# Rotation, first part, rest, second part and last part of queries and keys get a step each in an attention and expert-routing kernel

## What is computed

```python
q, k, v = (heads(wq, bq), heads(wk, bk), heads(wv, bv))
q = _apply_rope(q, cos, sin)
k = _apply_rope(k, cos, sin)
att = jnp.einsum('bhtd,bhsd->bhts', q, k) * scale
att = jnp.where(causal, att, jnp.float32(-jnp.inf))
att = jax.nn.softmax(att, axis=-1)
y = jnp.einsum('bhts,bhsd->bhtd', att, v)
...
x = _layernorm(x + attention)
probs = softmax(x @ gate_w.T); top 8 of 32 experts, weights normalised
x = _layernorm(x + sum over the 8 of  w_e * (u * silu(g)) @ down_w[e].T)
```

## Time and profile before

| | |
|---|---|
| median of three runs | 2444.79 us |
| lowest, highest | 2440.87, 2453.05 us |
| the profiled execution's own time | 2436.65 us |
| its span in the trace | 2434.7 us |
| mean granted TensorE clock | 0.941 of full speed |
| busy over the span | PE 83%, DVE 67%, ACT 64%, POOL 46% |

### The profile page before, as it was taken

The page is one execution under the profiler, slowest core; times in us unless marked ns, Lnnn a source line. Parts: engine busy times, 40 slices in busy tenths (PEclk is TensorE's granted clock), DMA queues, the critical chain, the costliest instruction groups (busy, mean ns, idle before and its releaser), DMA issues.

```text
span 2434.7 us, 57839 instructions
## 1 busy us (share of the span) xinstructions
PE 2024.7 (83%) x18031; PEld 1451.6 (60%) x18031; DVE 1641.3 (67%) x3492; ACT 1561.8 (64%) x3171; POOL 1125.8 (46%) x1110
## 2 busy tenths in 40 slices
PE   4888888888888888888779999998898997989780
PEld 3454544444544444445448788887787886778660
DVE  4677777777777677777635655655677775776673
ACT  2566665656645555555547677777787886878670
POOL 1005345543455345554353013002777757775775
PEclk7899999999989999989989999999899999999995
DMA  5456566656667666657847679888999998999893
GB/s 174 131 163 218 177 216 226 228 184 193 207 218 259 223 205 226 219 183 239 279 169 266 195 247 330 265 271 283 324 355 314 321 307 283 323 315 293 281 298 113
DMA packets 330817, 591.90 MB, mean 243 GB/s; under 512 B 47168, under 2 KB 168416, under 8 KB 328416
## 3 DMA queue, kind: packets, MB, share of 16 engines
q1 hardware_dynamic: 251232, 400.17, 50.6%
q0 software_dynamic: 53760, 159.45, 19.3%
q10 hardware_dynamic: 25536, 28.58, 3.6%
HBM read 326.68 MB, written 299.50 MB: 257 GB/s over the span
## 4 chain that ended last, share of the span: by engine, by line
PE 32%; POOL 18%; DVE 14%; issue 13%; DMA 11%; ACT 6%; SPq 4%; ACTq 1%; DVEq 1%; POOLq 0%
POOL stacks L759 16%; DMA qk_parts<-pbuf 4%; DVE mn L1484 3%; PE ps L876 3%; PE ps L935 3%; PE ps L1008 3%; PE ps L923 3%; PE ps L901 3%; PE ps L989 2%; PE ps L991 2%; PE ps L990 2%; DMA stacks<-qk_parts 2%; SPq L591 2%; PE ps L825 2%; ACT work L1143 2%
## 5 line engine op out<-in xcount | busy, mean ns | idle before, releaser
L1143 ACT ACTIVATE pT<-ps 128x1024 f16<-128x1024 f16 (+4 forms) x1408 | 825.5, 599 | 419.7 <-PE ps L925 287.4
L743 POOL DMA_INDIRECT x_sorted<-xhl,idx x512 | 532.4, 1040 | 415.2 <-DVE xhl L1555 263.7
L759 POOL DMA_INDIRECT stacks<-y_sorted,idx x512 | 522.7, 1021 | 396.7 <-DMA y_sorted<-work 196.3
L1484 DVE TENSOR_REDUCE mn<-ps 128x1 f32<-128x512 f32 (+3 forms) x704 | 416.0, 633 | 93.4 <-PE ps L903 89.0
L989 PE MATMUL ps<-pT,gu_hi 128*128 128x256 f16 x1536 | 425.4, 277 | 14.3 <-issue 7.9
L990 PE MATMUL ps<-pT,gu_hi 128*128 128x256 f16 x1536 | 424.8, 277 | 0.0
L991 PE MATMUL ps<-pT,gu_lo 128*128 128x256 f16 x1536 | 424.3, 276 | 0.0
L923 PE MATMUL ps<-stacks 99*128 99x512 bf16 (+3 forms) x1024 | 310.2, 317 | 67.1 <-ACT pT L1143 44.7
L901 PE MATMUL ps<-stacks 96*128 96x512 bf16 (+3 forms) x1024 | 290.8, 317 | 62.6 <-DMA stacks<-qk_parts 35.8
L1051 PE MATMUL ps<-dn,vx 128*128 x768 | 212.1, 276 | 80.6 <-DVE vx L1647 54.3
L925 PE MATMUL ps<-maskk,identb 128*128 128x128 bf16 x1024 | 232.9, 228 | 0.0
(11 more groups left out here) (229 smaller groups left out, 3634.0 us busy)
## 6 DMA issues: line engine op xcount, KB each, us to landing
y_sorted<-work SPq DMA_DIRECT2D x288, 256.0 KB
stacks<-qk_parts SPq DMA_DIRECT2D x128, 384.0 KB
x_sorted<-zeros_h SPq DMA_DIRECT2D x132, 288.0 KB
stacks<-x_sorted SPq DMA_DIRECT2D x88, 288.0 KB, 4.0
y_sorted<-yev SPq DMA_DIRECT2D x96, 256.0 KB
qk_parts<-pbuf SPq DMA_DIRECT2D x62, 384.0 KB
pT<-x_sorted SPq DMA_DIRECT2D x70, 288.0 KB
pbuf<-x_sorted SPq DMA_DIRECT2D x70, 288.0 KB, 5.3
```

The costliest lines, as they stand in the source:

```text
L743: pool.indirect_dma_start(xsort[g][:, :], bass.IndirectOffsetOnAxis(ap=at, axis=0), xhl_rows[:, t, :], None).then_inc(s_scat, 16)
L759: pool.indirect_dma_start(yg[:, r, k, :].bitcast(I32), None, ysort[g][:, :], bass.IndirectOffsetOnAxis(ap=at, axis=0)).then_inc(s_yg[r], 16)
L1143: return nc.scalar.activation(o, i, f, **k)
L1484: V.tensor_reduce(mn[:, tt, h0:h0 + nh], ps[:, odd_bank("max", at, m), 0:nh * n].rearrange("p (a n) -> p a n", a=nh), axis=AX.X, op=ALU.ma ...
```

## The change

The five operations get a step each. For queries: rotation in 3, first copy in 4, rest in 5, second copy in 6, last part in 7, write in 8 (before: 3, 4, 4, 5, 5, 6). For keys: 9, 10, 11, 12, 13, 14 (before: 8, 9, 9, 10, 10, 12). The keys' projection and `rope` go from steps 7 and 8 to 8 and 9, the load of the reciprocals from 10 to 11 and that of the numerators from 11 to 12. No instruction is added, removed or resized.

```diff
-SLOT_K = (7, 8)
-SLOT_PARTS = ((3, 4, 5, 6), (8, 9, 10, 12))
+SLOT_K = (8, 9)
+
+SLOT_PARTS = ((3, 4, 5, 6, 7, 8), (9, 10, 11, 12, 13, 14))
...
-SLOT_REC_IN = 10
-SLOT_NUM = 11
+SLOT_REC_IN = 11
+SLOT_NUM = 12
...
-                        if e == SLOT_PARTS[n][3] and nxt:
+                        if e == SLOT_PARTS[n][5] and nxt:
                             write_parts(i + 1, n)
...
-                        if e in SLOT_PARTS[n][1:3] and nxt:
-                            part_copy(i + 1, n, SLOT_PARTS[n][1:3].index(e))
+                        if e in SLOT_PARTS[n][1:4:2] and nxt:
+                            part_copy(i + 1, n, SLOT_PARTS[n][1:4:2].index(e))
...
-                            if e == SLOT_PARTS[n][1]:
+                            if e == SLOT_PARTS[n][2]:
                                 rest(i + 1, n)
-                            if e == SLOT_PARTS[n][2]:
+                            if e == SLOT_PARTS[n][4]:
                                 last_part(i + 1, n)
```

## The result

With the change the kernel takes 2487.07 us (median of 4 runs, 2469.44 to 2495.57), the kernel before beside it 2445.86 (4 runs): 1.016 times as long, 95% interval 1.009 to 1.022. Run again later beside 11 runs of the kernel before, it took 2481.26 against 2444.99, 1.0145 (1.0127 to 1.0164). So the change costs 36 to 41 us. The forecast was +10, and both times lie near or beyond the upper end of its range, 2482. The profiled execution took 2479.76 us with a span of 2477.8, 43 us over that of before.

The account below looks back on a forecast made before the run. It took the loop through the keys' write, the stack's load and step 20 to bound ten batches. 16 - 5 + 1 - 2 = +10 us on 2444.8 gave 2454.8 us, range 2422 to 2482.

Parts of the forecast that it names:

- What bounds the kernel: In ten batches, the loop of step 20, keys' parts, their write and the stack's load; PE waits 18.4 us for such loads.
- What the change removes: The ping-pong: PE's 4.44 us wait in step 10 and DVE's 2.19 before `last_part`; 2 to 2.5 us a batch if engine-bound.
- Queries' write: In batch 6 it starts 3.2 us later than at 534.97, at 538.1, behind two more steps' reductions.
- Its landing: The queries' write takes 9.9 us, landing at 548.0 in batch 6, so ACT's first keys copy waits 1.6 us.
- Rival B: Slower: step 8's 768 KB stack load ahead of the queries' write delays its landing 2 to 3 us; +30, 2475; 22%.
- Keys' write: In batch 6 it starts 3.1 us later, saves 1.4 beside fewer scatters, and lands 1.7 us later.
- the sum: Ten batches x 1.6 us = 16, less 5, plus 1, less 2: +10 us.
- credit of -5 for step 24: In five batches (3, 7, 10, 11, 14) a later stack only eats into step 24's wait of 1.0 us: -5.
- Numerators: Their load, now behind the row maxima, holds the division up 1 to 2 us; costed at nothing, step 20 not being due.
- The keys' projection takes as long a step later: Moved one step on, it costs nothing, PE being busy there in both.
- Rival C: Faster: the keys' write escapes the scatters and lands 2.1 us earlier; ten times, -21, 2424; 18%.
- Rival D: Nothing: bytes moved between steps 8 and 20, not the moment of issue, set the stack's arrival; 2445; 15%.

Follow-up runs that it names:

- g1: Kernel before with the keys' steps as changed (9 to 14), queries at their old steps, numerators' load at step 11: 2451.43 us against 2443.73, 1.0027.
- g2: Kernel before with only the keys' projection and everything behind it one step on, old ping-pong kept, write at 13: 2456.26 us against 2443.73, 1.0045.
- f3: Changed kernel with the queries' parts and write back at their old steps (3, 4, 4, 5, 5, 6): 2464.53 us against 2444.99 for the kernel before, 1.0077.
- g4: Kernel before with the keys' ping-pong undone (rotation 8, copies and parts 9 to 11), write kept at step 12: 2438.74 us against 2443.73, 0.9975.
- f1: Changed kernel with the queries' write issued ahead of step 8's stack load, same kernel as e1: 2479.30 us against 2444.99 for the kernel before, 1.0139.
- e1: Changed kernel with the queries' write issued ahead of step 8's stack load: 3323.27 us against 3342.85 for the kernel before, 0.994.
- e4: Changed kernel with the numerators' load back at step 11: 3328.61 us against 3342.85 for the kernel before, 0.995.
- f2: Changed kernel with the keys' first two parts in a buffer of their own in 12 of 14 batches: 2463.62 us against 2444.99, 1.0068.
- g3: Kernel before with only the keys' six pieces spread over steps 8 to 13 from the old start, write at 13: 2442.75 us against 2443.73, 0.9992.
- h1: Changed kernel with the numerators' load at step 11, e4 again: 3291.91 us against 3301.31 for the kernel before, 0.9965.
- h2: Changed kernel with the queries at their old steps, f3 again: 3291.94 us against 3301.31 for the kernel before, 0.9972.
- e3: Changed kernel with the queries at their old steps (3, 4, 4, 5, 5, 6): 3333.60 us against 3342.85 for the kernel before, 0.996.

## Why the prediction was wrong

**What bounds the kernel** was read rightly, as far as it went: the loop over the keys' write and step 20. PE's waits for stacks went from 18.4 to 41.7 us, where "towards 45" was forecast. What was overlooked is a second deadline on the same queue, step 12, for which the step-8 load comes just in time before the change (0.9 us of waits in all) and no longer does when the steps in front of it get shorter (g1, g2, f3: 39 to 45 us).

**What the change removes** held. PE's wait in step 10 of batch 6 is 1.15 us instead of 4.44 ("2 or less"), and DVE's wait before `last_part` is gone (28.5 us over all batches before); it now waits for ACT's first copy before `rest` instead, 39.7 us in 7 places. And the first of these comes of the later projection and copy (g2), not of the end of the ping-pong (g4).

**Queries' write** held: it starts 8.0 us before the end of the keys' rotation in batch 6 (546.41 to 554.38) where I had 538.1 to 546.4, 8.3.

**Its landing** is the step that failed. I took batch 8's 9.9 us as the price of the write, unchanged. It took 14.7 in batch 6 and 12.8 on average (9.2 before). Instead of 1.6 us, the copy stood 561.20 - 554.38 = 6.8 us past the rotation, 5.0 on average. The duration of a transfer was carried over from a row with nothing issued right ahead of it into a place where 768 KB go ahead. Rival B named just that, and its marker ("over 11 us") was met. The Trainium skill, "DMA: Bandwidth & Descriptors", section on queues, rings and completion order, says that each engine consumes one queue's descriptors in ring order. The traces agree as far as landings can show it: the transfer issued first lands first (load issued at 544.78 and landed at 552.5, write issued at 546.41 and landed at 561.12; in f1 the write lands 12.4 us and the load 16.2 us after the start of step 8). That all of the load's bytes go first, as I had put it, is more than that section of the Trainium skill states. And the order is only a part: putting the write first gave back 1.8 of the 3.6 us (2.8 us without scatters, e1 against e4). The other 1.8 come with the new place; scatters and DMA engines 94 to 95% busy were there at the old place too, so what they are made of stays open. B was priced at +30, 2475, and the measured 2481 to 2487 is beyond it; B as well took the keys' projection to be free, which cost 9 us, and the numerators. As a theory of what to do about it, B was wrong: the order in the queue is worth 2 us (f1), and 17 need an earlier write (f3) or another buffer (f2).

**Keys' write** was to start 3.1 us later and land 1.7 later. Counted from a batch's start it leaves 6.0 us later (23.1 - 14.3 from step 8, which comes 2.8 us earlier) and takes 8.4 us instead of 11.2, so it lands 3.2 later. That a later write is a shorter one held, with a larger saving than the 1.4 forecast; the start was off because the landing was. So **the sum**'s 1.6 us for ten batches became 2.7 us for each of thirteen (77.5 to 80.2), 35 of the 43 us between the two profiled executions, and the credit of -5 for step 24 came to -2.9 in the five batches named. Step 20 took 26 us more over batches 1 to 14, and step 12 is where the forecast had seen nothing: 6.2 us more in a batch.

**Numerators**, costed at nothing: some 12 us if f3 and g1 may be compared across two sets, next to nothing by DVE's waits in the changed kernel (1.7 us). This term stays open. **"The keys' projection takes as long a step later"** was right for PE's work and wrong for the time: 9 us (g1 to g3).

**Rival C** (faster) did not come about. Without scatters beside the write, near relatives of the change do gain 0.3 to 0.5% (h1, h2, e3, e4; the change itself was not run there), but in the sets of 2445 us the scatters are there. **Rival D** fell in its first half, though f1 shows its thought at work between two transfers. The direction was called, with 0.42 for slower; the range failed at its upper end because a landing over 11 us, B, was joined to no other loss.

## What to carry to other kernels

Price a transfer by what is ahead of it and beside it where it will be issued, not by its duration where it stood; if it frees a buffer for a copy on an in-order engine, all that is queued behind that copy is in the price too. When steps are shortened, list every transfer that is due in or behind them: one that came just in time will be waited for, here 5.6 us of a batch were gained before step 12 and more than that was waited off in it. Spreading a chain over more steps cost nothing here where its start stayed in place, even with its write one step later (g3); g4, which spreads it and keeps the write where it was, is the one version that beat the kernel before in the sets of 2445 us, by 5 us. What cost was starting the chain a step later (g1).

## What the runs showed of the hardware

The time SP needs to issue six transfers is no constant. In batch 6 it was 3.54 us for the queries' write before, 6.77 behind a load that was being moved, 5.09 with the write first (f1); on average over batches 2 to 14 it was 3.74, 4.96 and 4.33, and without scatters beside it 4.20 behind the load (e4) and 3.21 first (e1). And a program on one core can take 3300 to 3350 us or 2445 on the same chip, in different sets, with ACT and DVE standing up to 29 us at a time:

```profile
ACT pT L1144 <- remote: 395.9, 82, 28.8
```

That row is e4's. The stalls of the first half lie where POOL scatters: of the 59 waits over 7 us of ACT and DVE in batches 2 to 14 of e4, every one overlaps the batch's scatters, steps 2 to 5 take 45.9 us there and 12.4 in batch 1, before the first scatters. In the 2445 us sets the same scatters run and those steps take 12.0 us. What ends the waits, and why one set has them and another not, was not found. The sign of a change of 1% turned with it: one and the same kernel was 0.6% faster than the kernel before (e1) and 1.4% slower (f1).
